# Two matmuls of 256 moving columns in place of one of 512, in the turned score products of an attention stage

## The reference, cut to what matters

```
q = (x @ wq.T).reshape(B, S, 16, 16)        # 16 heads of 16 channels
k = (x @ wk.T).reshape(B, S, 4, 16)         # 4 key/value heads, each shared by 4 query heads
v = (x @ wv.T).reshape(B, S, 4, 16)
attn = einsum('bqhd,bkhd->bhqk', q, k) * scale
attn = where(causal, attn, -inf)
attn = softmax(attn, axis=-1)
out  = einsum('bhqk,bkhd->bqhd', attn, v).reshape(B, S, C) @ wo.T
h    = x + out
```

## Time and profile before

| | us |
|---|---|
| median of three runs | 2117.91 |
| lowest, highest | 2117.37, 2120.45 |
| the profiled execution | 2111.37 |
| its span, first to last instruction | 2109.7 |
| attention stage, first to last turned score product | 318.4 to 944.4 |

### The profile page before, as it was taken

The page is one execution under the profiler, slowest core; times in us unless marked ns, Lnnn a source line. Parts: engine busy times, 40 slices in busy tenths (PEclk is TensorE's granted clock), DMA queues, the critical chain, the costliest instruction groups (busy, mean ns, idle before and its releaser), DMA issues. The chain is left out here.

```text
span 2109.7 us, 50236 instructions
## 1 busy us (share of the span) xinstructions
PE 2036.1 (97%) x17544; PEld 1752.2 (83%) x17544; DVE 1347.3 (64%) x2818; ACT 1117.4 (53%) x2219; POOL 963.0 (46%) x1062
## 2 busy tenths in 40 slices
PE   7999989999999999989979999999899999999997
PEld 7999985666666666659979999999888888888886
DVE  7888954676777767765636776788654444444452
ACT  6777744666666666655543333344354444454542
POOL 0000002365565556556644444444245656565653
PEclk9999987999999999989989999999999999999998
DMA  8767711133233232229864444544344444545442
GB/s 294 264 260 267 261 59 31 62 104 96 92 108 110 87 106 96 78 92 305 300 218 144 148 151 142 175 150 151 104 96 109 95 111 95 112 96 111 96 83 30
DMA packets 134682, 289.62 MB, mean 137 GB/s; under 512 B 23026, under 2 KB 64755, under 8 KB 128243
## 3 DMA queue, kind: packets, MB, share of 16 engines
q1 hardware_dynamic: 84466, 177.25, 24.9%
q0 software_dynamic: 50048, 110.14, 20.3%
HBM read 187.17 MB, written 95.42 MB: 134 GB/s over the span
## 5 line engine op out<-in xcount | busy, mean ns | idle before, releaser
L1248 DVE TENSOR_REDUCE neg_max<-ring 128x2 f32<-128x512 f32 (+1 forms) x384 | 250.0, 681 | 106.4 <-PE ring L1734 106.1
L1041 POOL TENSOR_SCALAR_AFFINE_SELECT weights_diag<-weights_diag 128x512 f32<-128x512 f32 x256 | 158.3, 643 | 258.4 <-ACT weights_diag L1139 258.1
L2908 POOL DMA_INDIRECT out<-q_t,row_put x128 | 201.8, 1576 | 162.4 <-ACT q_t L2972 137.7
L3046 DVE TENSOR_TENSOR ex_hid<-ex_up_ps,gelu 128x512 f32<-128x512 f32 x128 | 86.9, 688 | 171.8 <-ACT gelu L2956 171.8
L2956 ACT ACTIVATE gelu<-ex_gate_ps 128x512 f32<-128x512 f32 x128 | 76.3, 596 | 187.3 <-PE ex_up_ps L62 187.3
L2379 POOL DMA_INDIRECT picked_rows<-results,lo_row_now x128 | 134.0, 1047 | 56.3 <-issue 29.8
L1139 ACT ACTIVATE weights_diag<-ring 128x512 f32<-128x512 f32 x256 | 138.5, 599 | 24.2 <-PE ring L1752 24.2
L60 PE MATMUL ex_down_ps<-ex_dn_lo,ex_hid_hi 128*128 128x256 f32 x512 | 145.1, 283 | 2.8 <-issue 2.8
L61 PE MATMUL ex_down_ps<-ex_dn_hi,ex_hid_lo 128*128 128x256 f32 x512 | 145.2, 284 | 0.0
L62 PE MATMUL ex_down_ps<-ex_dn_hi,ex_hid_hi 128*128 128x256 f32 x512 | 144.9, 283 | 0.0
L1049 POOL DMA_INDIRECT sorted_rows<-h_sb,row_now x128 | 126.8, 990 | 34.8 <-issue 31.3
(11 more groups left out here) (404 smaller groups left out, 7521.8 us busy)
## 6 DMA issues: line engine op xcount, KB each, us to landing
ug_raw<-in_w_ug SPq DMA_DIRECT2D x32, 1028.0 KB, 5.0
dn_raw<-in_w_dn SPq DMA_DIRECT2D x32, 640.0 KB, 5.2
q_t<-sorted_rows SPq DMA_DIRECT2D x136, 128.0 KB
moe_w<-in_expert_gu SPq DMA_DIRECT2D x16, 1024.0 KB, 4.8
results<-c0n POOLq DMA_DIRECT2D x33, 256.0 KB, 4.4
x_raw<-in_x_t SPq DMA_DIRECT2D x32, 256.0 KB, 5.1
c0n<-c SPq DMA_DIRECT2D x32, 256.0 KB, 4.3
c0r<-c SPq DMA_DIRECT2D x32, 256.0 KB
```

Of the source, the lines that this page charges most:

```text
L1041: nc.gpsimd.affine_select(part, part, [[0, G], [1, P]], ALU.is_ge, 0.0, base=0, channel_multiplier=-1).then_inc(kept_done, 1)
L1248: nc.vector.tensor_reduce(out, src, AX_X, ALU.max, negate=True).then_inc(max_done, 1)
L2908: nc.gpsimd.indirect_dma_start(out=out_rows, out_offset=bass.IndirectOffsetOnAxis(ap=at, axis=0), in_=eo[c][:, n, :], in_offset=None, comp ...
L3046: nc.vector.tensor_tensor(hid[f % 2][:], up_ps[f % 2][:], gelu[f % 2][:], ALU.mult).then_inc(hid_done, 1)
```

## The change

Each product of 512 moving columns becomes two of 256: query heads 0 and 1 (`c = 0`) into the first half of the bank, query heads 2 and 3 (`c = 1`) into the second. The outer loop runs over c and the inner one over the four row groups. The second half has `start` off and the first has `stop` off; they write different columns, so nothing is added up. The semaphore `turned_done[g]` is raised once for each bank as before, by the second half. Both halves use the same weights, the 17 x 128 slice of `k_t`, and these are loaded for each half. No wait is added or taken away, and no other engine's code changes.

```
-                for g in range(NKV):
-                    rows = slice(32 * g, 32 * g + HD + 1)
-                    nc.tensor.matmul(slot(2 * r, g)[:], k_t[n][rows, k * P:(k + 1) * P], q_t[n][rows, :, q * P:(q + 1) * P],
-                                     start=True, stop=True).then_inc(turned_done[g], 1)
+                half = 2 * P
+                for c in range(2):
+                    for g in range(NKV):
+                        rows = slice(32 * g, 32 * g + HD + 1)
+                        last = nc.tensor.matmul(slot(2 * r, g)[:, c * half:(c + 1) * half], k_t[n][rows, k * P:(k + 1) * P],
+                                                q_t[n][rows, 2 * c:2 * c + 2, q * P:(q + 1) * P], start=(c == 0), stop=(c == 1))
+                        if c == 1:
+                            last.then_inc(turned_done[g], 1)
```

## The result

The changed kernel takes 2125.9 us, the median of 6 runs (2122.2 to 2130.0), beside 2117.6 us for the kernel before, measured with it (6 runs). The ratio is 1.0038, with a 95% interval of 1.0023 to 1.0052. That is slower, by 8.3 us, where 0.6 us was predicted, and the median lies outside the range of 2114.5 to 2122.5. The profiled execution took 2124.6 us, its span 2122.9. That is 13.2 us over the span of before, but the profiled execution of before lay 6.5 us under its median; what is explained here is the 7.2 us by which the attention stage is longer (from the start of its first burst to that of its last, 319.2 to 951.9 us against 318.4 to 943.9). Of the other 6.0 us, 0.8 lie ahead of the stage and 5.2 behind it, where no instruction differs; the experiments come back to them. The granted clock is as before, and so is the shape of the stage.

What follows compares the result with a forecast made beforehand. PE was taken to bound the kernel. 96 bursts at 6 ns more each give 0.6 us, none hidden, so 2117.9 + 0.6 = 2118.5 us, with a range of 2114.5 to 2122.5.

Steps and rivals of the forecast that it cites:

- The bound: Attention stage: PE's queue sets the time, busy 566.93 of 570.00 us; one microsecond more between two starts adds one at the end.
- The cost of the burst: Each of 96 bursts: two more rounds add 4 to 10 ns, taken as 6 ns, 0.6 us in all.
- Loads in the open: Slower rival: each added round's weight load is exposed, 0.105 us, 20.2 us in all, 2138 us; chance 0.09 including a milder form.
- The step to the whole array: Faster rival, after each burst: the 0.11 us before full-array work shrinks, up to 10.6 us saved, 2107 us; chance 0.06.
- The step that failed: At the burst's end: `turned_done[g]` comes 1.12 us after the start before and after, so ACT's exponential keeps its distance; counted at nothing.
- PE now waits ... behind it: Sign that the prediction is wrong: PE waits at the start of a burst or behind it; no size given.
- The chances: Whole kernel: 0.85 for the forecast within 2115.5 to 2121.5 us, 0.09 for loads exposed, 0.06 for a shorter step after the burst.

Runs made afterwards that it cites:

- the quiet condition: Comparisons whose traces hold 29,300 to 29,500 semaphore events and nothing is late; the changed kernel measured 2114.0 us, ratio 0.9997, in one.
- the held one: Comparisons whose traces hold 23,700 to 24,100 semaphore events and r = 1 is late; the changed kernel's ratios were 1.0038, 1.0020 and 1.0019.
- one kernel in one held comparison: The changed kernel with its two loops exchanged, columns inside and row groups outside: 2118.4 us, ratio 1.0007.
- the two made to test it: Against the kernel before: only groups 2 and 3 split, 0 and 1 whole and first, 2115.4 us; only 0 and 1 split, issued behind group 2, 2118.1 us.

## Why the prediction was wrong

- **The bound** held. PE's queue sets the stage, and every 0.28 us between two starts stayed in the stage: 24 batches gave 7.0 us.
- **The cost of the burst** held: 5 ns for 6, rounds at 0.32, 0.54 and 0.75 us, shortest duration 373 ns. "Loads in the open" is refuted. Rounds two and three are 0.216 us apart with the second load of the same row group under them, as the row ahead of the prediction already said. The rule of the Trainium skill ("TensorE: Matmul & The Clock Gate", "The mechanism") that weight loads overlap with matmuls in flight only where the row group differs does not hold for this pattern. The step to the whole array did not shrink.
- **The step that failed** is "For the readers, `turned_done[g]` comes with the last pass of a bank ... So ACT's exponential ... starts at the same distance, and all that follows on ACT, POOL and DVE shifts with PE and not against it." The first half is an inference from modelled ends: 0.75 plus 0.374 is when the product is done, not when ACT is told. It came true in the quiet condition (1.16 us for 1.15). In the held one ACT was told later, in 26 of 32 bursts of r = 1 (batches 5 to 30): by 0.26 to 0.31 us in most, by 0.05 in batch 11 and by 0.72 in batch 30. So what followed on ACT did move against PE, and PE waited for it through group 3 of L1727. The text named "PE now waits ... behind it" as a way to be wrong, but gave it no price and no share in the chances.
- **The missing question** was what ACT's lateness would cost. I took the small entries of PE's waits for proof that nothing reaches PE. But group 3 of L1727 was already waiting for ACT in the kernel before. The burst of r = 1 lasts 1.32 us there, and the one of r = 0, without that wait, 1.15. The group started 0.19 us behind the one before it, and since the three other groups kept PE "busy", no view of waits counts it. With that read, a term "late exponential, one to one, r = 1 only" with a bound of 0.2 to 0.4 us in 32 batches would have put 6 to 13 us on the slow side. How late the exponential would come, no row ahead of the prediction could tell: that trace is a quiet one.
- **The chances** were too sure of it: 0.85 stood for the quiet condition, which three of six comparisons had. Of these one holds the changed kernel, and there the forecast of no change is right, 2114.0 against 2115.0 (as a time of its own, 2114.0 lies 0.5 us under the range). That the same kernel would take 1.0038 or 0.9997 by where it runs was in none of the rivals.

## What to carry to other kernels

Where an edit moves an increment to a later instruction, follow it to its reader and on to the next engine, and ask there for the slack; between row groups of TensorE read a burst's duration against its sisters', since a wait of one group does not show as idle time. Try to put the increment that someone waits for early in a burst; here one kernel in one held comparison speaks for it, and the two made to test it fell into quiet ones. Look at what indirect DMAs on POOL lie beside a semaphore without slack: 3 to 8 us went with that in the kernels with r = 1 split and 110 us in the one with the scatter moved. And when a loss of 0.3% doesn't come back with the same kernel, run the same kernel several times, on other chips too, before explaining it.

## What the runs showed of the hardware

- Increments at the end of four products whose modelled ends are 7 ns apart are raised 42.5 ns apart, in the order of issue (1409, 1452, 1494 and 1537 ns after the burst at 606.35, and 1135, 1177, 1220 and 1262 ns after the one at 603.57 in the kernel before).
- A semaphore was raised 0.27 to 0.74 us after its matmul's modelled end in 25 batches of the changed kernel, 0.5 to 0.6 us behind the end of a POOL indirect DMA, while PE's own work went on in time. With the scatter moved another one was raised 1.70 to 2.07 us late, 0.77 to 0.88 us behind the last of four such DMAs. Whether this happens differed between comparisons, and its cost for the same program from nothing to 5% (2116 and 2230 us).
- Row groups run on by themselves: the last matmul of group 3 of L1727 started at 609.67 us, after mask products of the other groups (from 609.46) that stand behind it in the program. With the two loops exchanged a burst of eight products took only 20 ns more.
- 1.6 us without a matmul went with a fall of the granted clock to 0.50 for 5.9 us of the work behind it. That made more of the 110 us than the wait did: PE's waits for L1340 are 36.1 us in all.
